# First tiles of a phase in a three-layer MoE kernel: one hand-over for four tiles, or one for each

## What is computed

```python
x = x + 0.5 * ffn(layernorm(x))     # MoE: 12 experts, top 3, 128 -> 512 -> 128, exact GELU
x = x + attn(layernorm(x))          # gate, decaying convolution over time, norm, gated MLP
x = x + 0.5 * ffn(layernorm(x))
# ffn: weights = softmax(top3(x @ Wg)); y = sum_k w_k * (gelu(x @ Wup[e_k] + bup) @ Wdown[e_k] + bdown)
```

## Time and profile before

| | us |
|---|---|
| median of 3 runs | 671.45 |
| lowest and highest run | 670.88, 675.17 |
| the profiled execution | 671.78 |
| its span | 670.0 |
| PE busy in it | 580.4 (87%) |

### The profile page before, as it was taken

The page is one execution under the profiler, slowest core; times in us unless marked ns, Lnnn a source line. Parts: engine busy times, 40 slices in busy tenths (PEclk is TensorE's granted clock), DMA queues, the critical chain, the costliest instruction groups (busy, mean ns, idle before and its releaser), DMA issues. The chain is left out here.

```text
span 670.0 us, 18238 instructions
## 1 busy us (share of the span) xinstructions
PE 580.4 (87%) x4678; PEld 537.5 (80%) x4678; DVE 356.4 (53%) x1637; ACT 414.7 (62%) x1254; POOL 421.6 (63%) x431
## 2 busy tenths in 40 slices
PE   5479999987969999899988999999996999999805
PEld 4358999987959887798878987778996999999702
DVE  6864445241107899976622699986661142323206
ACT  2336676774537787776745777877673666666404
POOL 1137777777767770357747777055774777777773
PEclk9758999998979999999997999999998899999957
DMA  9745666698578763357588875345767878777248
GB/s 247 207 130 147 182 206 207 182 179 250 179 213 253 210 196 113 111 165 209 159 235 235 243 212 165 111 139 161 207 192 206 254 214 239 224 217 232 65 111 227
DMA packets 127559, 127.92 MB, mean 191 GB/s; under 512 B 17257, under 2 KB 90784, under 8 KB 127460
## 3 DMA queue, kind: packets, MB, share of 16 engines
q1 hardware_dynamic: 111684, 99.26, 51.5%
q0 software_dynamic: 12992, 26.11, 13.8%
q10 hardware_dynamic: 2784, 1.38, 0.7%
HBM read 96.62 MB, written 30.79 MB: 190 GB/s over the span
## 5 line engine op out<-in xcount | busy, mean ns | idle before, releaser
L882 ACT ACTIVATE hT<-ps,BU 128x128 f32<-128x128 f32 x944 | 269.3, 370 | 130.3 <-PE ps L738 128.6
L738 PE MATMUL ps<-xT,WU 128*128 128x128 f32 x1888 | 259.3, 282 | 14.5 <-DMA WU<-in_L_ffn_Wup_dram 6.3
L738 PEld LDWEIGHTS ps<-xT,WU 128*128 128x128 f32 x1888 | 238.0, 197 | 27.6 <-issue 19.9
L749 PE MATMUL ps<-WD,hT 128*128 x1888 | 251.2, 277 | 1.5 <-DVE Ys L1296 1.2
L749 PEld LDWEIGHTS ps<-WD,hT 128*128 128x128 f32 x1888 | 231.1, 193 | 3.0 <-issue 2.8
L554 POOL DMA_INDIRECT xs<-XN,SX x144 | 148.4, 1030 | 103.3 <-issue 70.4
L1296 DVE TENSOR_TENSOR Ys<-ps,BD 128x128 f32<-128x128 f32 x236 | 68.0, 289 | 231.3 <-PE ps L749 223.2
L567 POOL DMA_INDIRECT YG<-ys,SY x144 | 149.3, 1037 | 60.3 <-issue 40.5
L541 POOL DMA_INDIRECT xl<-xn,SG x59 | 60.3, 1021 | 31.5 <-issue 16.9
L576 POOL DMA_INDIRECT yk<-Ys,row x59 | 59.1, 1001 | 19.9 <-issue 14.7
L960 DVE SCALAR_TENSOR_TENSOR X<-YG,WK,X 128x128 f32<-128x128 f32 x144 | 50.7, 352 | 17.8 <-DMA YG<-ys,SY 12.5
(11 more groups left out here) (210 smaller groups left out, 499.1 us busy)
## 6 DMA issues: line engine op xcount, KB each, us to landing
WU<-in_L_ffn_Wup_dram SPq DMA_DIRECT2D x236, 256.0 KB
ys<-Ys SPq DMA_DIRECT2D x39, 256.0 KB
xl<-xs SPq DMA_DIRECT2D x118, 66.0 KB
xl<-xs SPq DMA_DIRECT2D x59, 64.0 KB
WD<-in_L_ffn_Wdown_dram SPq DMA_DIRECT2D x12, 256.0 KB, 5.3
WD<-yk SPq DMA_DIRECT2D x12, 256.0 KB, 5.7
xs<-XN,SX POOLq DMA_INDIRECT x144
YG<-ys,SY POOLq DMA_INDIRECT x144, 3.2
```

What stands on the lines that cost most here:

```text
L738: x = e.matmul(HB[i % 2][:, c * P:(c + 1) * P], WU[i % NW][:, c * P:(c + 1) * P], xT[m % 2][:, j * P:(j + 1) * P], start=True, stop=True)
L749: x = e.matmul(YB[i % 2][:, 0:D], hT[i % 3][:, c * P:(c + 1) * P], WDf[:, bass.ds(r + c * P, P)], start=(c == 0), stop=(c == C - 1))
L882: x = e.activation(hT[i % 3][:, c * P:(c + 1) * P], HB[i % 2][:, c * P:(c + 1) * P], ACT.Gelu, bias=BU[:, bass.ds(b + c, 1)])
```

## The change

In phases 1 to 3 the first four tiles are now handled like those of phase 0: PE transposes tile 0 ahead of up(0), tile 1 ahead of up(1), tiles 2 and 3 ahead of up(2), each into a PSUM bank of its own; ACT copies each of them by itself, counted on `s_xh0`. The four loads of group 0 each have a semaphore of their own (`s_x1[j]`, where `load_rows` has g = 0). Group 1 of phases 1 to 3 is transposed and copied at k = 2 instead of k = 0. DVE still runs its `turn_x` (registers, and in phase 3 the target rows) for group 0 at the end of tile 58, waiting for the four semaphores in phase 3, and for group 1 at k = 2. Phase 0 keeps its order.

```diff
 def next_group(i):
     n, _, k = TILES[i]
-    if i in (0, 3):
-        return 1 if i else None
-    if k % 4 == 0 and k // 4 + 1 < NG:
+    if k == (2 if n else 3):
+        return NG * n + 1
+    if k and k % 4 == 0 and k // 4 + 1 < NG:
         return NG * n + k // 4 + 1
     if k == NTL - 1 and n + 1 < NPH:
         return NG * (n + 1)
...
+def firsts(i):
+    k = TILES[i][2]
+    return {0: [0], 1: [1], 2: [2, 3]}.get(k, [])
...
                 for j in range(size(g)):
-                    e.dma_start(xl[m % NXL][:, j, 0:DX[h]], xs[h][bass.ds(at[j], P), :]).then_inc(s_xl[m % NXL], 16)
+                    e.dma_start(xl[m % NXL][:, j, 0:DX[h]], xs[h][bass.ds(at[j], P), :]
+                                ).then_inc(s_xl[m % NXL] if g else s_x1[j], 16)
...
-            def turn_first(j):
-                ps = bank(("X", 0, 0, 0), j)
-                e.wait_ge(s_x0[j], 16)
-                e.transpose(ps[:, 0:P], xl[0][:, j, 0:D], ident[:]).then_inc(s_xp0 if j < 3 else s_xp, 1)
+            def turn_first(n, j):
+                m = NG * n
+                ps = bank(("X", m, j, 0))
+                e.wait_ge(*((s_x1[j], 16 * n) if n else (s_x0[j], 16)))
+                e.transpose(ps[:, 0:P], xl[m % NXL][:, j, 0:D], ident[:]).then_inc(s_xp0 if j < 3 else s_xp, 1)
...
-                e.wait_ge(*((s_xh, m) if m else (s_xh0, j + 1)))
+                e.wait_ge(*((s_xh, m - n) if k >= 4 else (s_xh0, 4 * n + j + 1)))
...
             for i in range(NI):
-                if i < 4:
-                    turn_first(i)
+                for j in firsts(i):
+                    turn_first(TILES[i][0], j)
                 up(i)
                 for x in downs(i):
                     down(x)
-                if next_group(i) is not None:
+                if next_group(i) is not None and next_group(i) % NG:
                     turn_x(next_group(i))
...
             for i in range(NI):
-                if i < 3:
-                    turn_first(i + 1)
+                n, h, k = TILES[i]
+                if k == 0:
+                    turn_first(n, 0)
+                if k < 3:
+                    turn_first(n, k + 1)
                 gelu(i)
```

More of the change, by code:

```diff
@@ L147, in ring @@
     for i in range(-1, NI):
-        if i >= 0 and next_group(i) is not None:
-            take(("X", next_group(i), 0, 0), 1)
+        if i >= 0:
+            for j in firsts(i):
+                take(("X", NG * TILES[i][0], j, 0), 1)
+            if next_group(i) is not None and next_group(i) % NG:
+                take(("X", next_group(i), 0, 0), 1)
         for step in SLOTS["P"][i]:
             take(step, RING[step[0]])
-        if i == -1:
-            take(("X", 0, 0, 0), 4)
     return used, last
@@ L288, in macaron_kernel @@
             "s_sg"))
-        s_x0, s_xp0, s_xh0 = [sem(f"s_x0{j}") for j in range(4)], sem("s_xp0"), sem("s_xh0")
+        s_x0, s_x1 = ([sem(f"{n}{j}") for j in range(4)] for n in ("s_x0", "s_x1"))
+        s_xp0, s_xh0 = sem("s_xp0"), sem("s_xh0")
         s_xg = [sem(f"s_xg{i}") for i in range(NXL)]
@@ L320, in drained @@
                     "A3": (s_n3, c), "A4": (s_e4, c), "A5": ((s_a5, s_u5)[u % 2], c), "A6": (s_e6, c), "A7": (s_X, c),
-                    "X": (s_xh, h) if h else (s_xh0, u + 1), "B": (s_bu, 1)}[kind]
+                    "X": (s_xh, h - h // NG) if h % NG else (s_xh0, 4 * (h // NG) + q + 1), "B": (s_bu, 1)}[kind]
         def landed(m):
@@ L327, in landed @@
                 return s_xg[m % NXL], 16 * sum(size(x) for x in range(m % NXL or NXL, m + 1, NXL))
-            return s_xl[m % NXL], 16 * sum(size(x % NG) for x in range(NG, m + 1) if x % NXL == m % NXL)
+            return s_xl[m % NXL], 16 * sum(size(x % NG) for x in range(NG, m + 1) if x % NXL == m % NXL and x % NG)
         def tables_of(n):
@@ L713, in turn_x @@
                     wd_at[(m, j)] = v
-            def turn_first(j):
-                ps = bank(("X", 0, 0, 0), j)
-                e.wait_ge(s_x0[j], 16)
-                e.transpose(ps[:, 0:P], xl[0][:, j, 0:D], ident[:]).then_inc(s_xp0 if j < 3 else s_xp, 1)
+            def turn_first(n, j):
[3 more added lines that the diff above has]
+                e.transpose(ps[:, 0:P], xl[m % NXL][:, j, 0:D], ident[:]).then_inc(s_xp0 if j < 3 else s_xp, 1)
                 if j == 0:
-                    e.wait_ge(*tables_of(0))
-                    for x, v in enumerate(table(e, eW[0], 0, HID * (E - 1))):
-                        wd_at[(0, x)] = v
+                    e.wait_ge(*tables_of(n))
+                    for x, v in enumerate(table(e, eW[n], 0, HID * (E - 1))):
+                        wd_at[(m, x)] = v
             def warm(count):
@@ L867, in turn_x, with turn_first @@
                 e.activation(xT[m % 2][:, 0:w], psum[USED[("X", m, 0, 0)][0][0]][:, 0:w], ACT.Copy).then_inc(s_xh, 1)
-            def turn_first(j):
-                e.wait_ge(*((s_xp0, j + 1) if j < 3 else (s_xp, 1)))
-                e.activation(xT[0][:, j * P:(j + 1) * P], psum[USED[("X", 0, 0, 0)][j][0]][:, 0:P], ACT.Copy
+            def turn_first(n, j):
+                m = NG * n
+                if j == 0:
+                    e.wait_ge(*tables_of(n))
+                    for x, v in enumerate(table(e, eB[n], 0, C * (E - 1))):
+                        b_at[(m, x)] = v
+                    if n:
+                        n2, g2 = (m - 2) // NG, (m - 2) % NG
+                        e.wait_ge(s_up, NTL * n2 + 4 * g2 + size(g2))
+                e.wait_ge(*((s_xp0, 3 * n + j + 1) if j < 3 else (s_xp, m + 1)))
+                e.activation(xT[m % 2][:, j * P:(j + 1) * P], psum[USED[("X", m, j, 0)][0][0]][:, 0:P], ACT.Copy
                              ).then_inc(s_xh0, 1)
@@ L889, in _ @@
                 side(step)
-            e.wait_ge(*tables_of(0))
-            for j, v in enumerate(table(e, eB[0], 0, C * (E - 1))):
-                b_at[(0, j)] = v
             e.wait_ge(s_bu, 1)
-            turn_first(0)
             for i in range(NI):
-                if i < 3:
-                    turn_first(i + 1)
+                n, h, k = TILES[i]
[3 more added lines that the diff above has]
+                    turn_first(n, k + 1)
                 gelu(i)
@@ L1274, in turn_x @@
                 if n == 3:
-                    e.wait_ge(*landed(m))
+                    if g:
+                        e.wait_ge(*landed(m))
+                    else:
+                        for j in range(4):
+                            e.wait_ge(s_x1[j], 16 * n)
                     dv.on(e.tensor_tensor(
```

## The result

The changed kernel takes 667.52 us (median of 20 runs, 666.15 to 671.44) against 671.55 for the one before (20 runs, 669.28 to 675.17): a ratio of 0.994, 95% interval 0.9928 to 0.9952, which is 4.0 us. So there is a gain, and the two comparisons put it at 2.4 and 4.0 us. The forecast was 669.7; the first measurement is about twice the 1.8 us it added up.

A forecast was written before the change was run, and what follows sets the result against it. PE's waits for loads at the starts of phases 1 to 3 were taken as on the path; gains 0.74 + 0.30 + 0.76 = 1.8 us off 671.78 gave 669.98, as median 669.7. The range was 666.3 to 673.4.

The forecast's parts named there:

- The starts are on the path, and the shift is handed on: Phases 1 to 3: PE's load waits, 15.2 us, delay each start; an earlier PE moves the next start by as much.
- Head start: Starts of phases 1 to 3: first load lands 1.55, 1.56, 1.89 us ahead of the fourth, taken whole.
- Holes: PE idle around the tile-by-tile copies at each later start: 1.23 us together, where before there were 0.73.
- Moved group at nothing: Group 1 of phases 1 to 3 moved to k = 2: costs nothing; 0.85 or 0.44 us if cover were gone.
- Phase 0 unchanged: Phase 0: taken to keep its order, so the forecast sum has no term for it.
- Clock, and the sum for each start: Fourth up of phases 1 to 3, clock rise unmoved: gains 0.74, 0.60 (half kept, 0.30) and 0.76 us.
- POOL's 1.87 us as the cap of phase 3: Phase 3: POOL waits 1.87 us beyond its pace for Ys, so no more can be kept from the third start.
- Loads together: Rival at later starts: four loads land together, 0.7 us slower, 672.2; chance 0.15, shared with gains swallowed by POOL and gathers.
- Whole head start: Rival at later starts: clock rises earlier or never falls, all 4.98 us comes through, 666.5; chance 0.18.
- Half clock for longer: Rival at later starts: half clock lasts 10.34 us as in phase 0, 2.6 us lost, 674.0; chance 0.17.
- The sum of PE's waits for `xl<-xs`: Sign of being right, PE over the whole span: these load waits fall from 15.2 us to about 10.2.
- The distance from issue to transpose: Sign at each later start: PE's first transpose about 1.6 us nearer the first load issue; no nearer would mean wrong.

The follow-up runs named there:

- e2: Changed kernel, but the first transpose of phases 1 to 3 waits for all four loads again: 673.06 us, ratio 1.0024 to the kernel before.
- e12: The changed kernel measured again, unaltered, beside fresh runs of the kernel before: 668.38 us against 671.37, ratio 0.9965.
- e3: Kernel before, with only group 1 of phases 1 to 3 transposed and copied at tile 2 instead of tile 0: 671.14 us, ratio 0.9993.
- e4: Kernel before, with only a semaphore per load, each tile transposed as it lands; one copy, group 1 at tile 0: 671.87 us, ratio 1.0009.
- e1: Changed kernel with phase 0 put back to its old order: 669.57 us, ratio 0.9968 to the kernel before.
- e10: Changed kernel plus 50, 12 and 12 unread transposes on PE behind the last down of phases 0, 1, 2: 668.59 us, 0.9951 to the kernel before.

## Why the prediction came out as it did

**The starts are on the path, and the shift is handed on:** right for the path, half right for the rest. e2 against the changed kernel (ratios 1.0024 and 0.994, or 0.9965 in e12) shows that the early landing is worth 4 to 5.6 us. But of 1.1, 2.8 and 2.6 us by which the fourth up comes sooner (means of the table above) the stages keep 0.8, 0.6 and 1.4.

**Head start (1.55, 1.56, 1.89 us):** too small. It was read off the issues and took the first load's flight as long as the fourth's. From first issue to first transpose it is now 1.89, 1.90 and 1.90 us where it was 3.94, 4.43 and 4.95: 2.05, 2.53 and 3.05 us. This pair of profiles flatters it; the means of four are 1.8, 2.0 and 2.6, so 6.4 us in sum against the 5.0 forecast.

**Holes (1.23 us):** right, 1.09 at phases 1 and 3 and 1.27 at phase 2.

**Moved group at nothing:** right about its own cost (e3), wrong about its part. I had named as its only price the loss of cover; e4 shows that without the move two of three starts wait about 1 us for the group's loads. That the change needs both parts is inferred from this.

**Phase 0 unchanged:** wrong, and an omission. I misread the diff: a tile is turned one place earlier there, and POOL, which I had not looked at in phase 0, was waiting for PE later in the phase. Worth 1.0 us by the stages, part of it the clock's, and anything from 0.2 to 1.9 by e1's ratio against the two of the changed kernel. The rows for it were in the trace: POOL's wait of 0.91 us for PE at 99.22.

**Clock, and the sum for each start (0.74, 0.30 after half, 0.76):** in the profile the fourth up gained 0.51, 3.79 and 1.78 us relative to the first issue. The first is near the calculated case: full clock was back 9.32 us after the first issue, before 9.00. The second is the rival in which the clock doesn't fall. At the third, full clock was back 9.30 us after the issue, before 10.67, so the assumption that the rise stays where it is failed there too.

By the means of four the fourth up gained 1.1, 2.8 and 2.6 us, 6.5 in sum, where the forecast had 0.74 + 0.60 + 0.76 = 2.1. This is the step that was most wrong: the head start was not eaten by half clock, because after the shorter wait PE mostly restarted at full clock. What lies behind the fourth up then took back more than half, 6.5 to 2.8, where the forecast took 0.30. The candidates are in the rows, the fifth tile's weights (1.66 us) and POOL's gathers (4.75 us of waits of DVE in phase 2); no run shows how the loss divides between them. The two errors point in opposite directions, and that the three starts end at 2.8 by stages, not far from 1.8, is luck.

**POOL's 1.87 us as the cap of phase 3:** what was kept (1.4) lies under the cap, but the waits did not vanish, so the reckoning behind the cap failed. In the changed kernel POOL still waits 1.20 and 1.10 us for Ys at 522.23 and 535.21; in this profile POOL itself started 5.54 us earlier (512.13 against 517.67), about as much as PE's fourth up (519.06 against 524.79).

**Rivals.** Loads together: refuted by e4. Whole head start, 666.5: of all cases the nearest to the first median (667.52), and nearer than the forecast about what reaches the fourth up (4.98 against 6.5 by the means; the forecast had 2.1). It is wrong that all of this comes through to the end. Half clock for longer: seen at e2's start of phase 1 and at e12's (all three ups at 2.05 us), not as the outcome. The Trainium skill's passage on short idle spells (TensorE: Matmul & The Clock Gate, A second HAM failure mode: psum-queue depth-cycling) agrees with e10, where the clock fell in a stretch of work with holes, but the outcome it was cited for didn't come. The prediction said that phase 0 agreed with it. It didn't show that: there the clock had been at half since before 34 us, so nothing fell.

**My signs.** The sum of PE's waits for `xl<-xs`, expected at 10.2 us, was 11.3, with 8.4 of it at phase 1: PE had finished phase 0 earlier and just waited longer. It was a bad sign. The distance from issue to transpose was a good one. Two signs of being wrong came: POOL's waits for Ys in phase 3 were still there (1.20 and 1.10), and DVE waited over 1.5 us for YG in phase 2 (1.83 and 1.77). The second fits the little that phase 2 kept; the first was a bad sign, as phase 3 kept most.

**Left open:** why phase 2 takes anything from 163.3 to 166.7 us in one and the same form (162.9 to 165.6 in the other), and so what its start is worth; where the gain between the fourth up and the end of a phase goes; what phase 0's order is worth by itself; and why e10, which put off the fall of the clock, gained nothing.

## What to carry to other kernels

When several transfers feed one step, look at the flight of the first one alone: it may be a good deal shorter than that of the last, so waiting for each by itself can give more than the distance between their issues. Ask whether the shorter wait changes the clock at which PE restarts; here that was worth more than the mis-read head start. Check what the engine meets next: an early start is lost if the next group of transfers is awaited ahead of the work that could hide it. And read a diff for each phase it touches, with the engines that hang on buffers there, since one surprise here was a tile moved by one place in a phase that seemed untouched.

## What the runs showed of the hardware

- A load of 64 or 66 KB from HBM let PE start 1.9 us after its issue when it was first of its burst, in the changed kernel's profile, and 1.9 to 2.65 us in the 24 such starts of all profiles. The fourth of the burst took 2.0 to 3.05 us in 18 starts (issue times of the fourth worked out as in the prediction).
- The clock can fall while PE is at work: in e10 it went to half about 2.6 us after PE had restarted from an idle time of 0.96 us, in a stretch of transposes and ups with holes of 0.4 to 0.5 us. In the changed kernel, after 1.40 us of idle time and similar holes, it stayed at full from 347 us on, and so it did in e12, the same kernel, after 0.97 us. At the third start it fell in both (at 510.60, after 1.55 us of idle time, and at 516.70, after 1.99).
- At the starts of phases 2 and 3 in those profiles, an idle time of PE of 2.0 to 4.5 us was followed by a first up at half clock in eight of eight cases, one of 0.95 to 2.0 us by one at full clock in seven of eight. The length doesn't settle it: in e2 and e10 a first up ran at full clock after 2.16 and 2.81 us.
